# Layer 0's grouped attention: where the next batch's keys, values and the mixing products stand among the tile slots

## The reference, cut to what matters

```
q = x @ Wq + bq                      # (8, 100, 512): 32 heads of 16
k = ctx @ Wk + bk                    # (8, 361, 128): 8 heads of 16
v = ctx @ Wv + bv
scores = q . k / sqrt(16) + mask     # four query heads to one key head
out = softmax(scores) @ v            # (8, 100, 512)
x = layernorm(out @ Wo + bo + x) * gamma + beta
```

## Time and profile before

| | us |
|---|---|
| median of three runs | 2772.2 |
| lowest, highest | 2767.01, 2772.35 |
| profiled execution | 2768.3 |
| its span, first to last instruction | 2766.5 |
| TensorE matmuls busy in the span | 2494.0 |
| VectorE, ScalarE, GpSimd busy | 1396.1, 1139.6, 1117.7 |

### The profile page before, as it was taken

The page is one execution under the profiler, slowest core; times in us unless marked ns, Lnnn a source line. Parts: engine busy times, 40 slices in busy tenths (PEclk is TensorE's granted clock), DMA queues, the critical chain, the costliest instruction groups (busy, mean ns, idle before and its releaser), DMA issues. The chain is left out here.

```text
span 2766.5 us, 37822 instructions
## 1 busy us (share of the span) xinstructions
PE 2494.0 (90%) x14008; PEld 2181.9 (79%) x14008; DVE 1396.1 (50%) x2343; ACT 1139.6 (41%) x2439; POOL 1117.7 (40%) x498
## 2 busy tenths in 40 slices
PE   7888479989998788899979999998998999999698
PEld 5666334578984456599879999988997899999698
DVE  4666621388884432233345666633333565664643
ACT  3777121223322311123455666632235565665321
POOL 2100322342212110262277878836224887876300
PEclk9999669999998899899989999999999999999899
DMA  7453601699972015143754545415275544542300
GB/s 232 115 124 76 213 13 52 183 248 240 236 183 83 0 61 172 57 165 132 266 174 131 161 144 169 153 46 199 102 254 171 168 144 142 163 142 94 112 31 24
DMA packets 215850, 385.68 MB, mean 139 GB/s; under 512 B 88740, under 2 KB 127676, under 8 KB 215028
## 3 DMA queue, kind: packets, MB, share of 16 engines
q1 hardware_dynamic: 215668, 383.28, 44.8%
HBM read 288.03 MB, written 103.35 MB: 141 GB/s over the span
## 5 line engine op out<-in xcount | busy, mean ns | idle before, releaser
L1777 PE MATMUL att_ring<-ca_pp,att_arena 128*128 128x400 f32 (+1 forms) x2304 | 439.3, 349 | 27.4 <-POOL att_arena L1859 15.5
L1777 PEld LDWEIGHTS att_ring<-ca_pp,att_arena 128*128 128x128 f32 (+1 forms) x2304 | 423.7, 192 | 36.7 <-POOL att_arena L1859 20.2
L1848 POOL TENSOR_TENSOR att_arena<-att_arena 128x1448 fp32r<-128x1448 f32 x64 | 212.2, 3315 | 255.4 <-ACT att_arena L1865 255.4
L1777 PE MATMUL att_ring<-att_arena,qk_wh 128*128 128x362 f32 x1024 | 257.4, 333 | 0.0
L2461 DVE TENSOR_TENSOR ca_yl<-att_ring,att_arena 128x400 fp32r<-128x400 f32 x256 | 146.6, 573 | 203.7 <-ACT att_arena L2420 203.7
L1859 POOL TENSOR_TENSOR att_arena<-state_X,att_arena 128x1536 fp32r<-128x1536 f32 x64 | 224.4, 3507 | 5.0
L1856 POOL TENSOR_TENSOR att_arena<-state_X,att_nothing 128x1536 fp32r<-128x1536 f32 x64 | 176.1, 2751 | 47.0 <-DMA state_X<-in_ctx 47.0
L1777 PE MATMUL att_ring<-att_arena,qk_wl 128*128 128x362 f32 x512 | 173.8, 339 | 18.8 <-POOL att_arena L2042 18.4
L1777 PEld LDWEIGHTS att_ring<-att_arena,qk_wh 128*128 128x128 f32 x1024 | 186.6, 193 | 0.0
L2420 ACT ACTIVATE att_arena<-att_ring 128x400 fp32r<-128x400 f32 x256 | 128.8, 503 | 95.0 <-PE att_ring L1777 94.8
L1871 ACT ACTIVATE att_kstage<-att_score,att_shift 100x362 f32<-100x362 f32 x256 | 143.8, 563 | 44.5 <-DVE att_shift L1884 44.4
(11 more groups left out here) (403 smaller groups left out, 6028.7 us busy)
## 6 DMA issues: line engine op xcount, KB each, us to landing
att_arena<-keys SPq DMA_DIRECT2D x64, 724.0 KB, 5.2
state_X<-in_ctx SPq DMA_DIRECT2D x64, 512.0 KB, 3.8
queries<-att_arena SPq DMA_DIRECT2D x16, 1600.0 KB
att_arena<-queries SPq DMA_DIRECT2D x64, 400.0 KB, 3.9
keys<-rec_stage SPq DMA_DIRECT2D x32, 724.0 KB, 4.4
keys<-att_kstage SPq DMA_DIRECT2D x32, 724.0 KB, 3.5
l_arena<-kept_value SPq DMA_DIRECT2D x176, 100.0 KB, 6.1
state_X<-in_ctx SPq DMA_DIRECT2D x64, 210.0 KB, 4.2
```

The costliest lines, as they stand in the source:

```text
L1777: issued = nc.tensor.matmul(out, x, y, start=(first and k == 0), stop=(last and k == count - 1))
L1848: self.nc.gpsimd.tensor_tensor(self.kl[:, n % 2].bitcast(F32R), self.kl[:, n % 2], self.kh[:, n % 2].bitcast(F32), ALU.subtract).then_inc( ...
```

## The change

The slots are moved, the values' products are cut finer, and SP's order is another:

- `make_keys` stands in slots 1 to 4 instead of 10 to 13. `make_values` makes two products a slot in slots 13 to 18 instead of four a slot in 15 to 17.
- Quad 1's mixing of the batch before moves from slots 7 to 9 to slots 6 to 8, its left-over columns to slot 9; quad 0's from 20 to 22 to 19 to 21, its left-over columns to slot 0 of the next batch. VectorE's copy of quad 0 moves from slot 24 to slot 2 of the next batch. `PIECES` is 1, so a mixing product still covers all 384 columns.
- After the last batch VectorE divides both quads behind its tile loop, not only quad 1.
- SP stores quad 0's output of b - 1 in batch b after the queries, then stacks the keys, then stores quad 1's output and packs the sums. The context of b + 2 waits for the values of batch b + 1, not of b.

```diff
--- before.py
+++ after.py
@@ -198,7 +198,9 @@
 
     RS, RM, RP, RT = 3, 6, 6, 3
     LAG = 5
-    KEY_AT, VALUE_AT, AV_AT = 10, 15, 20
+    KEY_AT, AV_LATE, VALUE_AT, AV_AT = 1, 6, 13, 19
+    PIECES = 1
+    WIDE = P * BLOCKS // PIECES
     NS = KV0 * HG * L // P
     Q_PART, K_PART = (1, 0, 0), (0, 1, 0)
     SPANS = [(0, 1), (1, 4), (4, B)]
@@ -386,16 +388,18 @@
                         sp.wait_ge(score_full, TILES * b)
                     stack_queries(b + 1)
                 if b:
+                    store_output(b - 1, 0)
+                if b + 1 < B:
+                    stack_keys(b + 1)
+                if b:
                     store_output(b - 1, 1)
                     pack_sums(b - 1)
-                if b + 1 < B:
-                    stack_keys(b + 1)
                 if b + 2 < B:
-                    sp.wait_ge(value_full, b + 1)
+                    sp.wait_ge(value_full, b + 2)
                     load_context(b + 2)
                 if b:
                     widen_inverse(b - 1)
-                store_output(b, 0)
+            store_output(B - 1, 0)
             store_output(B - 1, 1)
             sp.wait_ge(late_in, 16 * len(late))
 
@@ -547,15 +551,16 @@
                 if n < total and b + 1 < B:
                     if i == KEY_AT + CC + 1:
                         keep_key(b + 1)
-                    if i == VALUE_AT + 4:
+                    if i == VALUE_AT + 7:
                         keep_value(b + 1)
-                if n < total and i == AV_AT + 4:
-                    finish(b, 0)
-                if n < total and b and i == AV_AT + 4 - 13:
+                if n < total and b and i == 2:
+                    finish(b - 1, 0)
+                if n < total and b and i == AV_LATE + 3 * PIECES + 2:
                     finish(b - 1, 1)
                 if n < total and b and i == TILES - 2:
                     invert_sums(b - 1)
-            normalise(B - 1, 1)
+            for quad in range(QUADS):
+                normalise(B - 1, quad)
 
         @block.tensor
         def _(pe):
@@ -568,14 +573,14 @@
                 if c == CC - 1:
                     last.then_inc(key_full, 1)
 
-            def make_values(b, t):
-                if t == 0:
+            def make_values(b, k):
+                t, c = k // CC, k % CC
+                if k == 0:
                     pe.wait_ge(k_done, b + 1)
                 s0, rows = STILES[t]
-                for c in range(CC):
-                    last = nc.tensor.matmul(front[0:rows, t * P:(t + 1) * P], ctx[:, b % 2, c, s0:s0 + rows], Wv[:, c, :],
-                                            start=(c == 0), stop=(c == CC - 1))
-                if t == 2:
+                last = nc.tensor.matmul(front[0:rows, t * P:(t + 1) * P], ctx[:, b % 2, c, s0:s0 + rows], Wv[:, c, :],
+                                        start=(c == 0), stop=(c == CC - 1))
+                if k == 3 * CC - 1:
                     last.then_inc(value_full, 1)
 
             def turn_tile(n):
@@ -586,15 +591,16 @@
                     last = nc.tensor.transpose(turn[n % RT][:, t, :], probs[:, n % RP, t * P:(t + 1) * P], ident[:])
                 last.then_inc(turn_full, 1)
 
-            def attend(b, quad, t):
-                if t == 0:
+            def attend(b, quad, piece):
+                t, cols = piece % 3, slice(piece // 3 * WIDE, (piece // 3 + 1) * WIDE)
+                if piece == 0:
                     kept_tile(pe, TILES * b + 4 * BLOCKS * (quad + 1))
                     pe.wait_ge(v_done, b + 3)
                     if b or quad:
                         pe.wait_ge(y_done, QUADS * b + quad)
                 for j in range(4):
                     g = 4 * quad + j
-                    nc.tensor.matmul(mixed[32 * j:32 * j + 32, 0:P * BLOCKS], v[:, b % 2, t, g, :], turned[:, g, t],
+                    nc.tensor.matmul(mixed[32 * j:32 * j + 32, cols], v[:, b % 2, t, g, :], turned[:, g, t, cols],
                                      start=(t == 0), stop=(t == 2))
 
             def attend_left(b, quad):
@@ -618,8 +624,8 @@
             for c in range(CC):
                 make_keys(0, c)
             pe.wait_ge(value_weight_in, 16)
-            for t in range(3):
-                make_values(0, t)
+            for k in range(3 * CC):
+                make_values(0, k)
             pe.wait_ge(query_weight_in, 16)
             for u in range(len(UNITS)):
                 if u in (0, 2 * CC):
@@ -627,7 +633,7 @@
                 make_queries(u)
             pe.wait_ge(ident_in, 16)
             pe.wait_ge(query_low, len(UNITS))
-            for n in range(total + AV_AT - 10):
+            for n in range(total + AV_LATE + 3 * PIECES + 1):
                 b, i = place(n)
                 if n < total:
                     if i == 0:
@@ -651,17 +657,17 @@
                 if n < total and b + 1 < B:
                     if KEY_AT <= i < KEY_AT + CC:
                         make_keys(b + 1, i - KEY_AT)
-                    if VALUE_AT <= i < VALUE_AT + 3:
-                        make_values(b + 1, i - VALUE_AT)
-                if n < total and AV_AT <= i < AV_AT + 3:
+                    if VALUE_AT <= i < VALUE_AT + 6:
+                        for k in range(2):
+                            make_values(b + 1, 2 * (i - VALUE_AT) + k)
+                if n < total and AV_AT <= i < AV_AT + 3 * PIECES:
                     attend(b, 0, i - AV_AT)
-                    if i == AV_AT + 2:
-                        attend_left(b, 0)
-                past = i - (AV_AT - 13)
-                if b and 0 <= past < 3:
-                    attend(b - 1, 1, past)
-                    if past == 2:
-                        attend_left(b - 1, 1)
+                if b and i == 0:
+                    attend_left(b - 1, 0)
+                if b and AV_LATE <= i < AV_LATE + 3 * PIECES:
+                    attend(b - 1, 1, i - AV_LATE)
+                if b and i == AV_LATE + 3 * PIECES:
+                    attend_left(b - 1, 1)
 
 
 def one(t, b, pattern, **sizes):
```

## The result

| | us |
|---|---|
| before, median of 6 runs | 2770.79 (2767.01 to 2773.03) |
| changed, median of 6 runs | 2759.87 (2755.94 to 2763.81) |
| ratio | 0.9965, 95% interval 0.9951 to 0.9979 |
| changed, profiled execution; its span | 2763.81; 2762.0 |

The change makes the kernel 10.9 us faster. The profiled execution of the changed kernel is its slowest of six, and that of before is under its median, so the two profiles stand only 4.5 us apart. Layer 0's attention, up to the first product of its output projection, ends at 284.8 before and 279.9 after; what follows takes 2481.7 and 2482.1 us. The whole difference is in the stage that was changed.

The account below looks back on a forecast made before the run. SP's queue turn in layer 0's attention was taken as the bound, a 27.0 us loop through the context load. 2768.3 - 11.5 + 1.2 = 2758, or 2762 on the median's footing; 2761 given, range 2752 to 2774.

Parts of the forecast that it names:

- The likeliest case: Layer 0's attention: SP's loop through the context load, 25.5 to 28.2 us, sets the pace; chance 0.51.
- The walk: Batch starts followed through layer 0's attention: last batch starts at 232.7 instead of 244.2, 11.5 us gained.
- The kl gap: TensorE's 1.65 us wait at a batch's first value product; seven such waits go, 11.6 us.
- the key gap: TensorE's wait before a batch's first score: gaps of 1.63, 2.14 and 3.15 us go, with the clock loss behind them.
- The loop through the context: SP's turn from one context landing to the next: 27.0 us, stalling TensorE 1.7 us at slot 1 each time.
- The 4.7: Loop term in SP's queue: from a context's issue to the first `ga_wide` load, 4.7 us.
- The 10.8: Loop term in SP's queue: keys read back 10.8 us after the mask's issue, bounds 10.4 and 13.1.
- rival A: SP's turn is hidden, the loop under 25.3 us, TensorE sets the pace: 18 us gained, about 2754; chance 0.16.
- The clock: Granted clock 0.94 in the batch behind a 2.14 us gap before the first score; half of that loss priced, 1.7 us.
- The mixing products and the values' cut: Mixing moved by a slot: nothing, bound 0 to 0.5 us a batch; value products two a slot: no cost where TensorE paces.
- Rival D: Values' finer cut leaves TensorE waiting for ScalarE: 0.5 x 7 = 3.5 us, inside the range; no chance of its own given.
- The tail: Last batch: quad 0's division comes after the last tile copy and the last mixing waits for it; costs 1.2 us.

Follow-up runs that it names:

- the repeat: The changed kernel measured again without an edit, beside the other experiments: 2756.3 against 2765.8 us for the kernel before, ratio 0.9967.
- the early keys alone: The kernel before with only KEY_AT moved from 10 to 1; values, mixing and SP's order as before: 2768.2 against 2765.8 us, ratio 1.0006.
- The context's load first: The changed kernel with SP loading the context of b + 2 at the head of batch b, not at its turn's end: 2757.9 us, ratio 0.9974 to before.
- the loads on GpSimd: The changed kernel with the widened inverses' eight loads and the wait before them moved from SP's to GpSimd's queue: 2746.0 us, ratio 0.9934 to before.

## Why the prediction was right

*Time and way.* 2761 was forecast and 2759.9 measured; on the chip of the experiments the gain was 9.4. The likeliest case held, with its mechanism. The walk came true up to the context of batch 4: asked for at 125.5, there at 127.7 (forecast 124.9 and 126.8). TensorE's own pace was 24.8 us and not 25.3, but the first key product stands 2.1 us behind the batch's start and not 1.3, and the two errors nearly cancel. The last batch, forecast for 232.7, starts at 232.8 in one profile and 237.2 in the other, so in the first pair of profiles the stage is only 4.9 us shorter, where 10.3 were forecast, and in the repeat 9.3. That the median came within 1.1 us is better than the sum deserves: turns differ by up to 3.9 us, and the later layers by more.

*The kl gap, the key gap*: both gone, as put. But they can't be summed as gains: the early keys alone show that the first is worth nothing by itself.

*The loop through the context.* Forecast 27.0, measured 27.0, 27.1 and 29.9 in one profile and 27.3, 26.0 and 28.0 in the other. Its terms in the first: keys read back 10.8 after the mask, measured 10.9, 10.6, 10.4, 12.3 and 10.9; context's issue to the wide loads 4.7, measured 4.4, 4.5, 4.4 and 6.3; the row sums' wait 1.5, measured 1.1, except once 1.7.

The 4.7 was right in size partly by luck. It came from a turn in which SP hardly waited for VectorE and the inverses' round trip took 4.0; in the changed kernel SP first waits 1.2 to 2.5 us for the reciprocals, and these, in three turns of five, for the packed sums; the round trip behind it takes only 2.3 to 3.3. The prediction said of the packed sums only that VectorE's wait lies inside TensorE's stall; that it also stands in SP's turn was left out. The 10.8 is 8.1 of issuing and 2.7 of waiting for the keys, measured as 8.2 and 2.7, 8.2 and 2.4, 7.7 and 2.7, 7.2 and 5.0, 7.3 and 3.6: the sign "over 3 us for the keys" did not follow from the prediction's own sum and was seen in two turns of five. "Under 2 for the row sums" held (1.7 at most).

The old turn of 27.3 us, which the prediction set against rival A, was the shortest of four: the contexts' loads issued at 95.88, 126.26, 155.43, 182.69 and 213.60 make turns of 30.4, 29.2, 27.3 and 30.9.

Of the two sections of the Trainium skill's "DMA: Bandwidth & Descriptors" that the prediction weighed, "Anatomy of one DMA" with its near constant 2.0 us gave an estimate of 10.1 and a loop of 26.3. The trace does not agree with it here: the keys' wait is 2.4 to 5.0 us for the same two writes, and the 10.1 was passed in all five turns. It fits the other, "Queues, rings and completion order", by which rings are consumed in order, with the keys behind what was issued ahead of them; no run took that away from the keys alone, so the reason is not shown.

*What is the bound.* The context's load first and the loads on GpSimd tell "the context's place" from "SP's turn": only the second gained, 10.3 us. Rival A, TensorE at its own pace, forecast 18 us for the case that SP's turn is hidden; with the loads on GpSimd it was 19.7.

*The clock.* A wait of 2.18 us cost 6% of granted clock in its batch, as the 2.14 us before, and one of 2.01 did too; one of 1.85 stands in a batch at 0.94 in the second profile, one of 0.97 in a batch at 1.00.

*The mixing products and the values' cut*, put at nothing. No run moved the mixing products alone. The values' cut is worth 0.44 us a batch once TensorE sets the pace; it was not tried where SP does. Rival D had its sign the wrong way round: where TensorE sets the pace the finer cut spares it time.

*The tail* was mis-sized: 1.2 forecast, 2.0 measured (from the last batch's start to the first projection 40.7 before, 42.7 in both profiles after): the last mixing starts 28.9 us after the batch instead of 27.2, so 1.7 later, and takes 4.1 instead of 3.8.

*Left open*: why single turns take 2 to 3 us more (key wait 5.0, context landed 6.1 after its issue); no run took that apart.

## What to carry to other kernels

Where a queue written by hand carries several round trips a turn, add up its turn before filling gaps on the engines: if the turn is as long as the batch, a gap that is filled comes back at the next thing that the queue delivers. Count in the turn the waits for an engine that itself waits for one of the queue's transfers. Put each wait of the queue behind everything that is ready earlier; one wait of 4 to 5 us a turn for an engine, in front of ready transfers, cost 20 us here over the stage. Moving a round trip and its loads to the queue of an idle engine was worth about as much (7 to 10 us) as the whole rescheduling (9.4), and the two add up.

## What the runs showed that I had not expected

SP's issue of the same transfers does not always take the same time: four outputs took 2.4 us in most turns, 3.35 in the turn shown above and up to 3.8 in others, and a context's load 1.84 instead of 0.42 in the earlier trace rows. In the changed kernel's two turns with slow outputs ahead of the keys (3.31 and 3.35) the keys' wait was short, 2.7 and 2.4; with quick outputs (2.4) it was 2.7, 5.0 and 3.6. That would fit a queue that holds up its issuer when it is full, but what decides it no run shows. And the same later layers, untouched, took from 2476.3 to 2490.5 us in the ten profiles of the experiments, a spread wider than most effects here.
